# A decoder on one core: rows go through the two Mamba layers in pairs, fewer plain steps, VectorE's small work beside any step

## What is computed

```python
out = x
for i in range(2):                       # two Mamba layers
    u, z = split(out @ in_w[i].T)        # 512 channels each
    u = silu(causal_dwconv(u))           # 4 taps
    dt, B, C = split(u @ xp_w[i].T)      # 16, 64, 64
    dt = softplus(dt @ dtw[i].T + dtb[i])
    for each time step t:                # the selective scan, 64 states a channel
        h = h * exp(dt_t * A) + (dt_t * u_t) * B_t
        y_t = sum over states of h * C_t
    out = ((y + u * D_skip) * silu(z)) @ out_w[i].T
x = layernorm(x + out)
x = layernorm(x + attention(q=x, k=v=ctx))
x = layernorm(x + experts(x))            # top 2 of 8, 256 -> 1024 -> 256, relu
```

## Time and profile before

| | us |
|---|---|
| median of 3 runs | 3252.25 (3250.26 to 3255.61) |
| the profiled execution | 3255.16 |
| its span, first to last instruction | 3253.4 |
| steps, first scan's start to last scan's end | 35.0 to 3039.7 |
| behind the last scan | 3039.7 to 3253.4 |
| granted TensorE clock, mean | 0.967 |

### The profile page before, as it was taken

The page is one execution under the profiler, slowest core; times in us unless marked ns, Lnnn a source line. Parts: engine busy times, 40 slices in busy tenths (PEclk is TensorE's granted clock), DMA queues, the critical chain, the costliest instruction groups (busy, mean ns, idle before and its releaser), DMA issues.

```text
span 3253.4 us, 59651 instructions
## 1 busy us (share of the span) xinstructions
PE 2873.8 (88%) x21906; PEld 2620.1 (81%) x21906; DVE 2914.1 (90%) x2038; ACT 2623.7 (81%) x6098; POOL 2663.1 (82%) x1317
## 2 busy tenths in 40 slices
PE   6889899998988899888988899989998989899676
PEld 4888888887888788787888788888897878888566
DVE  6999999999999999999999999999999999899410
ACT  6878888887889788887979799898989879788322
POOL 4989999888989899888989898888988888878311
PEclk8999999999999999999999999999999999999788
DMA  3254442222222222222222244424352334644086
GB/s 108 95 169 157 167 147 70 66 62 74 71 68 62 67 72 70 64 67 71 61 76 59 68 148 152 129 80 157 102 180 94 103 111 157 196 156 135 31 276 210
DMA packets 285448, 358.33 MB, mean 110 GB/s; under 512 B 100555, under 2 KB 180436, under 8 KB 284773
## 3 DMA queue, kind: packets, MB, share of 16 engines
q1 hardware_dynamic: 281202, 343.75, 33.5%
q0 software_dynamic: 3072, 8.39, 0.8%
q10 hardware_dynamic: 882, 2.38, 0.2%
HBM read 303.70 MB, written 50.73 MB: 109 GB/s over the span
## 4 chain that ended last, share of the span: by engine, by line
PE 33%; ACT 24%; POOL 14%; DVE 14%; issue 12%; DMA 2%; SPq 1%; POOLq 0%; DVEq 0%; ACTq 0%
POOL hC L1107 12%; ACT dA L1320 12%; PE psY L1665 9%; DVE h L1352 9%; PE psG L1604 7%; PE psX L1646 5%; ACT xs L1291 4%; PE psX L1636 4%; PE psG L1691 3%; DVE psX L1342 3%; PE psX L1604 2%; ACT gT L1162 1%; DMA w_up<-in_w_exp 1%; ACT scratch L1159 1%; PE psX L1628 1%
## 5 line engine op out<-in xcount | busy, mean ns | idle before, releaser
L1107 POOL TENSOR_TENSOR hC<-h,cb 128x1024 f32<-128x1024 f32 x1024 | 2404.0, 2371 | 374.7 <-DVE h L1352 336.5
L1352 DVE TENSOR_TENSOR_SCAN h<-dA,psX 128x1024 f32<-128x1024 f32 (+1 forms) x1101 | 2300.4, 2126 | 102.7 <-ACT dA L1320 35.9
L1320 ACT ACTIVATE dA<-dt,negA 128x255 f32<-128x255 f32 x4096 | 1720.0, 505 | 158.1 <-DVE h L1352 156.6
L1665 PE MATMUL psY<-ident,hC 128*128 128x128 f32 x8192 | 1088.3, 277 | 13.0 <-POOL hC L1107 10.8
L1665 PEld LDWEIGHTS psY<-ident,hC 128*128 128x128 f32 x8192 | 948.1, 143 | 25.3 <-POOL hC L1107 21.8
L1646 PE MATMUL psX<-diag_b,dtuT 128*128 128x128 f32 x4080 | 516.0, 281 | 54.9 <-DVE h L1352 52.8
L1646 PEld LDWEIGHTS psX<-diag_b,dtuT 128*128 128x128 f32 x4080 | 490.0, 195 | 87.7 <-issue 82.8
L1342 DVE TENSOR_TENSOR psX<-dtu,psX 128x1024 f32<-128x1024 f32 x411 | 496.8, 1209 | 19.5 <-PE psX L1628 18.9
L1636 PE MATMUL psX<-ident,xs 128*128 128x128 f32 x2864 | 388.4, 280 | 111.3 <-ACT xs L1291 69.5
L1291 ACT ACTIVATE xs<-dtuT,bT 128x512 f32<-128x512 f32 x716 | 476.8, 719 | 0.2
L1636 PEld LDWEIGHTS psX<-ident,xs 128*128 128x128 f32 x2864 | 326.6, 143 | 165.2 <-ACT xs L1291 91.7
(11 more groups left out here) (219 smaller groups left out, 2043.8 us busy)
## 6 DMA issues: line engine op xcount, KB each, us to landing
cb<-c_dram SPq DMA_DIRECT2D x256, 512.0 KB
w_up<-in_w_exp SPq DMA_DIRECT2D x173, 256.0 KB
w_down<-in_w_exp SPq DMA_DIRECT2D x173, 256.0 KB
diag_b<-b_dram SPq DMA_DIRECT2D x255, 128.0 KB, 3.6
x_slots<-got SPq DMA_DIRECT2D x32, 512.0 KB, 4.8
y_slots<-got SPq DMA_DIRECT2D x32, 512.0 KB, 5.0
dA<-in_w_exp SPq DMA_DIRECT2D x39, 256.0 KB, 5.0
h<-in_w_exp SPq DMA_DIRECT2D x39, 256.0 KB, 5.0
```

The source lines that it names most:

```text
L1107: eng.tensor_tensor(hC[i % NHC][:, :, :], h[i % NH][:, :, :], cw.to_broadcast([P, KI, L]), ALU.mult).then_inc(times_c, 1)
L1320: made = eng.activation(dA[j % NA][:, c, 1:L], dt[n % 2][:, c, 1:L], ACT.Exp, scale=negA[:, JOBS[n][0], c, s:s + 1])
L1352: made = eng.tensor_tensor_scan(h[i % NH][:, part, :].rearrange("p c t -> p (c t)"), dA[i % NA][:, part, :].rearrange("p c t -> p (c t)"), ...
L1665: made = eng.matmul(psY[:, tc, c * P:(c + 1) * P], hC[i % NHC][:, c, tc * P:(tc + 1) * P], ident[:, :], start=s == 0 and c == 0, stop=s == ...
```

## The change

The jobs come in pairs: (0, 0), (0, 1), (1, 0), (1, 1), (0, 2), (0, 3), (1, 2), (1, 3) and so on to (1, 6), (1, 7). Jobs 1 to 8 have 18 P, 23 T and 23 M, the last seven 26, 25 and 13. Over the 1024 steps this makes 358 P, 378 T and 288 M where there were 411, 358 and 255. VectorE's pieces may stand beside any step but the last.

```diff
-JOBS = [(0, 0)]
-for _b in range(1, ROWS):
-    JOBS += [(0, _b), (1, _b - 1)]
-JOBS.append((1, ROWS - 1))
+JOBS = []
+for _b in range(0, ROWS, 2):
+    JOBS += [(0, _b), (0, _b + 1), (1, _b), (1, _b + 1)]
...
-LATE = "PTPMPTPTPMTPTPT" * 4 + "PTPM"
+MID = "PMTPMTPMTMT" * 5 + "PMTPMTPMT"
+LATE = "PTMPT" * 12 + "PTMP"
...
-KINDS = FIRST_JOB + EARLY * 9 + LATE * (NJ - 10)
+KINDS = FIRST_JOB + MID * 8 + LATE * (NJ - 9)
...
-                limit["DVE"] = at["DVE"] + 2500 if i + 1 < STEPS and not is_turned(i + 1) else 0
+                limit["DVE"] = at["DVE"] + 2500 if i + 1 < STEPS else 0
```

## The result

| | before | after |
|---|---|---|
| median of 4 runs (us) | 3253.73 (3250.26 to 3255.61) | 3274.18 (3268.28 to 3280.44) |
| ratio after to before | | 1.0066, 95% interval 1.0046 to 1.0087 |
| profiled execution, its span | 3255.16, 3253.4 | 3280.44, 3278.7 |
| first to last scan | 3004.7 | 2986.0 |
| behind the last scan | 213.8 | 256.1 |

The changed kernel is slower by 0.66%, some 20 us, where I had forecast 12 us faster. The steps became 18.7 us shorter (forecast 45), the part behind them 42.3 us longer (forecast 33), and the first scan starts 1.6 us later: +25.3 us in the span.

The account below looks back on a forecast made before the run. VectorE was taken to bound the steps, busy 96% of them. Steps -67 + 22 = -45 us and +33 behind them gave -12 from 3252.25: 3240 us, own range 3226 to 3254, 8 in 10 3215 to 3268.

Parts of the forecast that it names:

- Kinds: In the steps: 53 plain steps become turned, each 1.26 us less on VectorE's path, -67 us (bounds -67 and 0).
- VectorE beside any step: Small VectorE pieces, now allowed beside turned steps, are the same pieces and delay nothing else: cost nothing.
- Waits, +22: In the steps, waits of about 130 us grow by 22: 6 for GpSimd, 16 for ScalarE's and TensorE's shorter recovery.
- GpSimd's floor: Jobs 1, 2 and 6 can't get shorter than GpSimd's work and idle time: near 170 us, GpSimd at 97%.
- Pairs as the cause of the six tiles: The paired job order starts group 1's tiles 52 steps later, so six tiles come behind the last steps, where none did.
- Behind the steps, +33: After the last steps: row 7's chain 42 us later, -11 from a faster clock, +2 for copies: +33 us (+14 to +50).
- Dropped fillers: In the steps, 447 TensorE fillers are dropped: costs nothing, though a rule on the clock speaks against it.
- TensorE becomes the bound: Rival, chance 0.18: jobs 10 to 15 follow TensorE, +11 us there; steps -12, behind them +33: 3273 us.
- Cheap tiles: Rival, chance 0.18: six tiles behind the steps run at 7.25 us each, row 7's chain 25 us late: 3223 us.
- the signs that I named against me: Wrong if the steps end before 2985 or after 3020, or the stretch behind them is under 230 or over 265 us.

Follow-up runs that it names:

- Any step alone: Kernel before with one line changed, VectorE's small pieces allowed beside turned steps too: ratio 1.0091, 1.0068 to 1.0115.
- pairs alone: Kernel before with only the order of the jobs changed, in pairs: ratio 1.0010, 0.9996 to 1.0025.
- late kinds alone: Changed kernel with the old kinds up to job 8 and VectorE's pieces beside plain steps only: ratio 1.0065, 1.0040 to 1.0090.
- early and late kinds: Early: changed kernel with the old kinds from job 9 on, pieces beside any step, 1.0035. Late: the run of late kinds alone, 1.0065.

## Why the prediction was wrong

It missed the change in the profiled span by 37 us, -12 against +25. By its steps:

- *Kinds, -67.* The count is right: 53 products are gone, and at the nominal times that is -67.2. But a turned step is not always 2.18 us: behind a T step an M step takes some 2.32. The new strings bring such pairs in, and their 12 us are among the waits below.
- *VectorE beside any step, "I cost it at nothing".* This is the step that failed, and the largest part of the 37: the pieces take 30.6 us more, 27 without the gates that are booked with them. 20.2 of it are the same operations, longer, because they wait for a GpSimd instruction that runs when they start; 6.0 is idle time before two residuals. I counted the same pieces in another place, and took an operation's duration as its own property. It depends on what GpSimd does at that moment. The kernel before already showed it: L1402 has a mean of 216 ns where the like L1404 has 174, so a few waited. With two-input pieces kept beside plain steps the small operations are back at the 105.4 us of before. Any step alone, costed at nothing, came out 0.91% slower.
- *Waits, +22.* The size came out, 21.5, by another way, so this is luck. I had 6 for GpSimd's floor and 16 for a slower recovery over all jobs. What came is 11.0 of listed idle time, where the last eighth of the jobs gained and the other eighths lost, and some 12 in the pairs of a T and an M step. The waits before the 128x1024 scans, for which I had said near 120, are 114.0.
- *GpSimd's floor.* Jobs 1 and 2, near 170, came out at 171.8 and 170.5, but with GpSimd busy 93 and 94%, not 97; job 6, by the stall above, at 180.5.
- *Pairs as the cause of the six tiles.* Wrong: pairs alone leaves the end as it was, late kinds alone makes it 33.6 longer.
- *Behind the steps, +33.* The mechanism was right, the size 9 us too small. The chain came 47.9 us later, not 42: a tile takes 11.1 to 12.5 us, where I took 11.1, and the sums stood 28 us behind the one before, not 24. The clock was 0.92, 1.00 and 0.85 where it had been 0.52 and 0.50, but that and the tiles beside the chain gave back 5.6, where I had 9. The estimate that I worked out from the Trainium skill, "DMA: Bandwidth & Descriptors", section "Anatomy of one DMA - SWDGE (gpsimd) path", gave waits of 1.3 us; 1.48 is measured. Its 10.6 us a tile I can't derive again: 11.1 less the two waits of the earlier trace rows and plus two of 1.3 is 10.0.
- *Dropped fillers.* The granted clock of the steps is 0.97, before 0.98; costing them at nothing holds within that.
- *The rivals.* The time is within 2 us of "TensorE becomes the bound" (3273), by another mechanism, which says nothing for it: its jobs 10 to 15 should have grown by 11 us and followed TensorE. They shrank, from 1180.0 to 1160.1 us, and in job 11 TensorE is busy 173.2 of 188.3 us, 92%. "Cheap tiles" falls with 11 to 12.5 us a tile. None of the rivals spoke of a piece's own length.

One of the signs that I named against me came: the steps end at 3022.6, past 3020. The other, a stretch behind them under 230 or over 265, did not (256.1).

## What to carry to other kernels

A rule that keeps small work beside certain steps may be guarding a port, not only an order: before moving an operation, look at what the neighbour on the shared ports does at the new place, and see whether a few of its instances are already longer than the rest. The kernel before lost some 10 us that way itself. When the order of kinds changes, look at which pairs are new, and not only at the counts: a fill that just fits behind one kind can miss behind another, by too little for any list of waits. Room that one kind of step gives is used by several (small pieces, preparation, tiles); taking it shows up where the last of them is due, here at the ends of jobs and of the program. And where work is left over behind the last step, issue the chain that the end depends on first and put the rest into its waits: it was worth 0.6% here.

## What the runs showed of the hardware

- A 128x16 tensor_tensor or tensor_scalar of VectorE between SBUF tensors, put beside GpSimd's work 42 times, took 1.59 us at the median, up to 1.94 and 2.22, and each ended 28 to 38 ns behind the GpSimd instruction that ran when it started. A reciprocal (0.227) and a tensor_reduce (0.144) of the same tensor never waited.
- A matrix fill starts 0.15 us behind the scan that frees its tile, lasts 2.02 us, and the next scan starts 0.04 us behind it (medians of 85 pairs): 2.20 us, just over the 2.18 from one scan's end to the next.
- GpSimd's multiply was not lengthened: 2371 ns before, 2370 after.
- Open: the waits of early and late kinds are +22.3 and +14.5 apart and +21.5 together.
- Open: the kinds of jobs 1 to 8 with small pieces beside plain steps only, without anything else, were not tried; the cost of the late preparation alone is therefore known only from kernels that have the ports' cost too.
